# The order in which eight attention groups are taken: the last short group but one moves behind the long ones

## The reference

```
x = x + attn0(layernorm(x)); x = x + ffn0(layernorm(x))
x = x + attn1(layernorm(x)); x = x + ffn1(layernorm(x))
attn: att = q @ k.T / 4 (+ alibi), causal; w = softmax(att); out = (w @ v) @ Wo
ffn1: wq = w.astype(float8_e4m3fn); down(silu(gate(x)) * up(x))
```

## Time and profile before

| | us |
|---|---|
| median of three runs | 449.85 |
| the profiled execution's own time | 446.99 |
| its span | 445.3 |
| TensorE busy | 397.3 |
| VectorE busy | 310.2 |
| ScalarE busy | 244.2 |
| GpSimd busy | 178.3 |

### The profile page before, as it was taken

How to read it: one execution, slowest core, us unless ns; L and a number is a source line. 1 busy time by engine, 2 the same in 40 slices (tenths; PEclk the granted TensorE clock), 3 DMA queues, 4 the chain that set the end, 5 groups by cost and what they waited for, 6 DMA issues and landing times.

```text
span 445.3 us, 14589 instructions
## 1 busy us (share of the span) xinstructions
PE 397.3 (89%) x6360; PEld 205.2 (46%) x6360; DVE 310.2 (70%) x630; ACT 244.2 (55%) x361; POOL 178.3 (40%) x255
## 2 busy tenths in 40 slices
PE   5898988999998888999799998888999988888997
PEld 4355743343334237544367555433333342365476
DVE  7865889999997116521744558999999971178883
ACT  3433556678788963221100442666887879735950
POOL 8416022403214134478682000234362553453770
PEclk9998989999999989999999999999999999999999
DMA  6069200000000000200100242100000000000002
GB/s 202 30 209 283 67 30 4 4 4 4 4 3 5 2 2 16 68 3 10 62 0 0 79 140 82 64 3 6 3 3 5 1 5 2 1 2 0 2 24 72
DMA packets 14889, 16.77 MB, mean 38 GB/s; under 512 B 1868, under 2 KB 14090, under 8 KB 14826
## 3 DMA queue, kind: packets, MB, share of 16 engines
q1 hardware_dynamic: 13730, 12.83, 9.1%
q0 software_dynamic: 544, 2.49, 1.8%
q10 hardware_dynamic: 552, 0.53, 0.4%
HBM read 8.27 MB, written 1.05 MB: 21 GB/s over the span
## 4 chain that ended last, share of the span: by engine, by line
PE 50%; DVE 24%; ACT 9%; POOL 8%; issue 5%; DMA 3%; SPq 1%; ACTq 0%; DVEq 0%; POOLq 0%
DVE mx L1327 17%; PE ps L846 10%; ACT prob L1210 8%; PE ps L792 7%; PE ps L1008 4%; PE ps L983 4%; PE ps L1044 4%; PE ps L1088 4%; PE ps L830 3%; PE ps L723 3%; PE ps L907 3%; PE ps L978 2%; DMA kS<-alibi_tail 2%; POOL oT L595 1%; POOL prob L632 1%
## 5 line engine op out<-in xcount | busy, mean ns | idle before, releaser
L1327 DVE TENSOR_REDUCE mx<-ps 128x1 f32<-128x512 f32 (+3 forms) x320 | 181.4, 628 | 27.3 <-PE ps L802 23.8
L1210 ACT ACTIVATE prob<-ps,s_exp 128x1024 f32<-128x1024 f32 (+1 forms) x192 | 163.3, 900 | 54.7 <-PE ps L830 53.9
L632 POOL TENSOR_SCALAR_AFFINE_SELECT prob<-prob 128x256 f32<-128x256 f32 x128 | 52.1, 411 | 168.3 <-ACT prob L1210 167.8
L792 PE MATMUL ps<-kS,qS 64*32 64x512 f16 (+11 forms) x1536 | 102.1, 321 | 15.7 <-DVE mx L1327 10.2
L846 PE MATMUL ps<-prob,v 128*32 128x512 f32 (+3 forms) x768 | 83.6, 507 | 2.0 <-POOL prob L632 1.4
L830 PE MATMUL ps<-qS,kS 64*32 64x512 f16 (+3 forms) x1528 | 76.8, 329 | 7.4 <-ACT prob L1210 6.6
L792 PEld LDWEIGHTS ps<-kS,qS 64*32 64x32 f16 x1536 | 35.5, 89 | 94.9 <-DVE mx L1327 80.5
L798 PE MATMUL ps<-mask_q,identb 64*32 64x32 bf16 (+1 forms) x1024 | 46.8, 180 | 0.0
L802 PE MATMUL ps<-mask_q,identb 64*32 64x64 bf16 (+1 forms) x512 | 41.6, 194 | 0.0
L830 PEld LDWEIGHTS ps<-qS,kS 64*32 64x32 f16 x1528 | 29.6, 90 | 24.1 <-ACT prob L1210 18.1
L978 PE MATMUL ps<-xnT,gu0T 128*128 128x512 f32 x80 | 34.9, 593 | 0.0
(11 more groups left out here) (156 smaller groups left out, 549.4 us busy)
## 6 DMA issues: line engine op xcount, KB each, us to landing
qS<-parts SPq DMA_DIRECT2D x24, 128.0 KB, 2.1
kS<-parts SPq DMA_DIRECT2D x24, 128.0 KB, 2.2
out<-x SPq DMA_DIRECT2D x8, 128.0 KB, 1.7
oT<-in_L_ffn_gate_w POOLq DMA_DIRECT2D x1, 768.0 KB, 4.9
oT<-in_L_ffn_up_w POOLq DMA_DIRECT2D x1, 768.0 KB, 4.7
parts<-in_L_ffn_down_w POOLq DMA_DIRECT2D x1, 768.0 KB, 5.5
prob<-in_L_ffn_wq_down SPq DMA_DIRECT2D x1, 704.0 KB, 6.2
prob<-in_L_ffn_wq_gate SPq DMA_DIRECT2D x1, 640.0 KB, 4.6
```

Of the source, the lines that this page charges most:

```text
L632: nc.gpsimd.affine_select(out=square, in_=square, compare_op=ALU.is_ge, fill=0.0, base=0, pattern=[[0, 2], [1, P]], channel_multiplier=-1) ...
L792: mmi = nc.tensor.matmul(span[r:r + STRIP, 0:seen], qS[own, c, pair, qt * P + r:qt * P + r + STRIP], kS[own, pair, key0:key0 + seen], star ...
L1210: nc.scalar.activation(prob[:, n % 3, pair::G // 2, off:CH], ps[:, 2 * (m % 2):2 * (m % 2) + 2, off:CH], ACT.Exp, scale=s_exp[:, L:L + 1]) ...
L1327: ins = nc.vector.tensor_reduce(mx[:, slot, qt, us[0]:us[-1] + 1, part], src, AX_X, ALU.max)
```

## The change

The table's third entry (2, 0), the first-half queries of the third set of heads, moves to the seventh place. The long groups of the four sets move up by one place each. W8_DOWN_AT stays at 3.

```diff
-CGS = [(0, 0), (1, 0), (2, 0), (0, 1), (1, 1), (2, 1), (3, 1), (3, 0)]
+CGS = [(0, 0), (1, 0), (0, 1), (1, 1), (2, 1), (3, 1), (2, 0), (3, 0)]
```

## The result

The changed kernel takes **456.55 us** (median of 4 runs, 455.74 to 457.54) against 449.58 before (4 runs, 447.51 to 450.31): ratio 1.0164, 95% interval [1.0124, 1.0203]. It is slower by more than the runs scatter; whether by as much as 2% the interval leaves open. The profiled execution took 457.54 us, 10.6 more than that of before; the medians differ by 7.0.

What follows compares the result with a forecast made beforehand. VectorE was taken to hold layer 1's first six groups, ScalarE the last two. Order +0.2, wait +7.7 and clock +1.6 gave +9.5: 456.5 from the profiled execution, 459.3 from the median; forecast 458.5 us, 8-in-10 range 453 to 463.

Steps and rivals of the forecast that it cites:

- Part 2: Layer 1, first long group: GpSimd waits for L1311, then rounds; TensorE stalls 9.2 us; net +7.7 us, ends 5.5 and 9.5.
- Little is won back: Layer 1, stretches behind the stall: held by VectorE with about 1 us slack each, so little of the stall is recovered.
- Part 3: TensorE's clock after the stall in layer 1: one low-clock piece, +1.6 us, ends 0 and 3.2.
- Part 1: Group order in both attentions: same pass pairs in another order, about +0.1 us per layer; bounds together -2.4 to +3.
- the prediction's own signs: Profile signs of being wrong: wait before L846 under 5 us, or layer 0 moving by over 2 us either way.
- my straight line: Layer 1, last long group: interpolation between stretches with 4 and 28 max items gave 17.2 us, taken as 17.1.
- The sum: Whole kernel: +0.2 for order, +7.7 for the wait, +1.6 for the clock, together +9.5 us.
- the faster tail: Rival, last long and moved short group at ScalarE's pace: 5.3 us saved in all, 441.7 or 451 with stall; chance 0.04.
- the shallower loss: Rival, layer 1 stall: VectorE slack and empty tail recover part, clock does not fall; 451.5 to 454.5 us, chance 0.14.
- The deeper loss: Rival, layer 1 stall: clock stays low for two pieces and banks refill slowly; 461 to 464 us, chance 0.11.
- The wait that isn't there: Rival, GpSimd in layer 1 has its count earlier, so only the order is left; 447 to 450 us, chance 0.06.

Runs made afterwards that it cites:

- e5: Changed kernel plus 72 useless matmuls in TensorE's wait ahead of the L846 of step 12 in layer 1: 455.37 us, ratio 1.0179 to before.
- e2: Kernel before, old order, with L1311 (VectorE's preparation of the down weights) one turn later (W8_DOWN_AT = 4): 456.16 us, ratio 1.0216.
- e3: Changed kernel where GpSimd still waits for L1311's count ahead of step 12 but rounds the quarters ahead of later groups: 450.45 us, ratio 1.0068 to before.
- e1: Changed kernel with L1311, VectorE's preparation of the down weights, one turn earlier (W8_DOWN_AT = 2): 447.42 us against 446.81 before, ratio 1.0022.
- e4: Changed kernel plus 56 useless matmuls in TensorE's wait ahead of the L846 of step 12 in layer 1: 456.09 us, ratio 1.0174 to before.
- e6: e1 plus two useless matmuls ahead of each max item 20 to 43 of both layers: 455.34 us, ratio 1.0184 to before.
- e8: e1 with the max pass paced 3 entries past a turn in place of 5 (TURN_AHEAD): 451.85 us against 447.85 before, ratio 1.0067.
- e7: Kernel before plus two useless matmuls ahead of each max item 20 to 43 of both layers: 457.00 us, ratio 1.0233.

## Why the prediction was right

- **Part 2, the wait: right in mechanism and size.** The L846 of step 12 began 22.35 us into its stretch against 13.33 before, 9.0 later; forecast 9.2. The turn's copy was forecast 8.7 later without the clock, and e5 measures 8.7 for the wait as a whole. e2 shows that the two counts alone make it, e3 that the rounding is 5.3 of it.
- **Little is won back: right.** The stretches behind are 18.13, 18.13, 16.34, as without the wait in e1 (18.12, 18.12, 16.34).
- **Part 3, the clock: near in size, open in its rule.** 1.1 to 1.45 measured by e4 and e5 for 1.6 forecast. The forecast told waits apart by their length. Both waits of 8.47 us (after, e2) did bring a fall, but so did 1.93 us of idle in e4, while 3.17 us in e3 and 2.8 us in the earlier trace rows did not.
- **Part 1, the order: near in sum by luck, wrong in its terms.** Forecast was +0.1 in each layer. The profiles give +1.6 in layer 1, the long stretch's 10.14 and the moved 0.94 set aside, and -2.2 in layer 0. The last long stretch took 16.34 where I took 17.1: eleven more max items cost nothing beside ScalarE's 14.69, and my straight line between two stretches with different bounds was the wrong tool. The moved short group took 7.09 (7.2 forecast). The second stretch took 11.16 at full clock in layer 0 (11.1 forecast). The first took 12.5 to 13.1 where I took 11.2. In layer 0 its clock was 0.86, and the old first stretch had 0.84. In layer 1 it was 0.64 to 0.74, where the earlier trace rows shows 1.00. I had costed that opening by VectorE alone.
- **Layer 0 broke one of the prediction's own signs.** It was to stay within 1.5 us, and over 2 us was named as a sign of being wrong: it moved by 2.2, from 111.6 to 109.4. 1.6 of that is the last group without its low piece (9.23 to 7.66). The old order shows that piece in both of its profiles without filling (before and e2), the new order in none of its profiles. Whether the order moves it is not shown. Against e2's layer 0 (110.4) the difference is 1.0.
- **The sum.** 9.5 was forecast. The profiled executions differ by 10.6: 8.7 less 0.94 for the wait, 1.45 for the clock, 1.6 and -2.2 for the rest of the two attentions, and 1.8 between them, where the low piece at 216.3 lies. That last one was in no term. It isn't that execution's alone: it stands in the profiles of the changed kernel, e1, e4 and e5, and not in those of e3, e6, e8, before and e2 (e7 has one at 221.3). Why is open. The medians differ by 7.0 only, since the profiled execution of before lies 2.6 under its median and that of after 1.0 over its own. That the forecast of 458.5 came within 2 us of 456.55 so owes something to terms that cancel.
- **Slips in the working, none of which moved the forecast.** GpSimd was to idle some 20 us; the chain of part 2 itself gives 16 (from 309.88 to 331.37 less 5.37), and 16.2 was measured. The bounds of part 1, -2.4 to +3, are narrower than the ends of its own terms: 16.4 and 6.29 alone give -3.0, and the rival of the faster tail -5.3. Nearly all of the shallower loss (451.5 to 454.5) lies within 4.5 us of 449.85, where only half of it was counted.
- **The rivals.** The shallower loss is out: e5 and e1 put the wait at its full size. The deeper loss is out by the time, though the clock did stay low for two pieces (322.1 to 328.9 us): 3.65 of these 6.8 us lay in the wait, where TensorE had nothing to do. The wait that isn't there and the faster tail are out with it, though the tail rival had one grain of truth: the last long stretch does run at 16.34 with 15 items beside it.

What stays open is why the clock falls in the opening of layer 1 in the new order. It fell there in all six profiles of that order that have no filling in the opening and ran near their usual time (after, e1, e3, e4, e5, e8), and in neither of the old order (before, e2). In e1 the fall came 2.56 us behind the first exponential. Until then TensorE's busy time is the same in both orders, the instructions are not (59 and 41 matmuls); before, then e1:

```profile
278.97:281.53 2.56, 1.63 (x59) 0.93 (x51) 2.49 (x8) 2.12 (x2) 0.78 (x2) 1.00 0.49 155
```
```profile
278.67:281.23 2.56, 1.59 (x41) 0.63 (x41) 2.49 (x8) 2.12 (x2) 0.78 (x2) 1.00 0.49 156
```

Fewer and wider matmuls stand there, and the clock falls behind them. That they cause it was argued, not shown. No long wait preceded the fall: TensorE's longest idle time in that window was 0.62 us. And in the profile of after it came at 277.7 us, in the work ahead of the first exponential, whose 22 max items both orders place alike. The runs give the size only roughly: at one granted clock of 0.980 to 0.981, four runs of the kernel before average 448.8 us and six of e1 446.8, while most runs of before beside them had 0.988 or more and none of e1 did. That suggests that the new order by itself would save some 2 us, and that the lower clock takes them back. No run without filling shows the new order at 0.988 or more.

## What to carry to other kernels

When a table sets the order of work, look for everything that is tied to a position in it by a number or by a property of the entry. Here a count was given at position 3 and taken at the first long group, and the table moved one of them. A side job that rides on an engine's idle time was free here only while the count it waits for came well ahead; when it came late, the wait and the job's whole length (5.4 us) fell on the engine that waited for GpSimd's next instruction. The distance between giver and taker is worth reading off the order before any time is summed.

## What the runs showed of the hardware

- Behind the wait, the low clock put 1.1 to 1.45 us on the path beside the 8.7 us of the wait itself (stretches of 28.03 in e4 and 28.38 after, against 26.93 in e5). Filling 6.3 us with matmuls, which left 1.93 idle, did not prevent the fall; filling 8.0, which left 0.17, went without one.
- The length of TensorE's idle time alone did not tell whether its clock fell: it fell behind 1.93 us (e4) and with no idle time over 0.62 us in the 2.56 us before (e1, 281.2 us), and stayed at 1.00 behind 3.17 us (e3) and 2.8 us.
- Two matmuls of the full array (128*128, 256 columns) ahead of each of 24 items, 0.39 us a pair in the timeline of e6, went with times 8 to 10 us longer over two layers in both orders. The array's own tiles there (64*32) overlap: in that timeline four matmuls of 512 columns take 0.40 us together and one alone 0.39. Whether the filling costs by breaking that overlap was not tested.
- Runs of one kernel follow the granted clock: of the kernel before, one run at 0.996 took 444.29 us and the four at 0.980 to 0.981 took 448.45 to 449.30.
